# Attention and routed experts on one core: GpSimd's indirect transfers get compute operations between them, and TensorE signals a values product only once a query group

## The chip, the cores and the metric

The kernel runs on one core of a Trainium2 chip. A core has TensorE (PE), VectorE (DVE), ScalarE (ACT), GpSimd (POOL) and SyncE (SP), each with its own in-order program; they meet through semaphores. Transfers run on 16 DMA engines: SP and ACT issue plain ones, GpSimd issues the indirect ones (rows picked by a list of indices). The metric is the device time of the core in microseconds (us), median over runs; less is better.

## The reference

The input x is (1, 2048, 128), float32. It is layer-normalised, and two branches are added to x.

```python
xn = layernorm(x)
# attention: one head of 128, though scaled by 1/sqrt(8)
q, k, v = split(xn @ w_qkv.T); s = q @ k.T / sqrt(8)
attn = softmax(s) @ v @ w_proj.T + b_proj
# routed experts: 8, the best 2 for each token
h = xn @ W_in + b_in
top-2 of softmax(h @ W_gate + b_gate), renormalised to sum 1
eout[e] = relu(h @ W1[e] + b1[e]) @ W2[e] + b2[e]
ffn = (sum of the two experts' outputs by weight) @ W_out + b_out
out = x + attn + ffn
```

## The kernel before

**Tiling.** The 2048 tokens are NT = 16 tiles of 128. Attention goes by six groups of queries, of 256, 256, 512, 512, 256 and 256 (`GROUPS`). A group of 512 takes 16 steps, one of 256 takes 8, with two key tiles each; steps are numbered through, and s counts them from the fourth group on (`BASE_B` = 32). In a step TensorE makes the scores into one of three banks (`scores`), ScalarE takes the exponential (`step`: `ph` in rounded form and `pf` in full from the third group on, only `pf` before), VectorE takes the remainder `pl` (`low`), and TensorE multiplies by the values two steps later (`values(i - 2)`). Beside that, the maxima of the next group's scores are found by pairs: `pair` on TensorE, `pair_max` on VectorE, 4, 8, 8, 4 and 4 pairs, put at given steps by `PAIR_STEP`.

**Stages.** After normalisation and projection VectorE finds each token's two experts and its two rows in a table sorted by expert (`slots`). The first three groups of attention run while GpSimd sends each token's row of h into this table in HBM. Then the experts run as MT = 39 tiles of 128 rows, and the results go to a second table. Then the last three groups run, while GpSimd fetches each token's two rows of results (`z`), ScalarE multiplies the first by its gate (`weigh`, line 495), VectorE adds the second times its own (`combine`, line 742), and a block of four tiles is transposed, projected and added to x (`moe_transpose`, `cT_copy`, `moe_project`, `moe_add`, at the steps of `BLOCK_AT`). Product j is put at the step s given by `weighed_at`, 5 + 13(j+1)//8: s = 6, 8, 9, 11, 13, 14, 16 and so on up to 31.

**GpSimd's order.** 16 bias additions of one tile each to x (line 320), then the wait for `slots`; 16 indirect transfers (line 342, tiles 0 to 7 twice); the first four copies of an expert's weights into `wst` (line 334); 16 more indirect transfers; the 35 other copies, each when its buffer is free; then 32 indirect fetches (line 365).

**Signals.** TensorE raises `st_done` after each scores product, `pv_done` after each values product, `max_done` after a pair, and `q_done`, `row_done`, `out_done`, `proj_done`, `cT_done` and `wo_done` after what their names say. ScalarE's `step` waits for `st_done` and, because `ph`, `pf` and `pl` have three buffers, for `pv_done` of three steps back. TensorE's own order has values(i - 3) ahead of scores(i).

Of the kernel before, what the change touches and what calls it, by code (L numbers as in the profile page):

```python
# [7 lines left out]
ALU = mybir.AluOpType  # L8
# [4 lines left out]
def attention_moe_kernel(nc, x, w_qkv, w_proj, b_proj, w_in, b_in, w_gate, b_gate,  # L13
# [43 lines left out]

    BY_DVE = [2, 2, 3, 3]
    NORMED = [sum(BY_DVE[:r + 1]) for r in range(NR)]

    def group_of(i):
        return max(g for g in range(NG) if FIRST[g] <= i)
# [12 lines left out]
    with ctx:  # L75
# [199 lines left out]
        @block.gpsimd  # L275
        def _(pool):
            pool.memset(ident[:, 0:P], 0.0).then_inc(Z["consts"], 1)
            pool.memset(xn[:, :, 0:1], 1.0).then_inc(Z["consts"], 1)
            pool.memset(wvT[:, D:D + 2], 0.0).then_inc(Z["consts"], 1)
            pool.wait_ge(Z["consts"], 3)  # L280
            pool.affine_select(out=ident[:, 0:P], in_=ident[:, 0:P], compare_op=ALU.not_equal, fill=1.0,
                               base=0, pattern=[[-1, P]], channel_multiplier=1).then_inc(Z["consts"], 1)
            pool.wait_ge(Z["consts"], 4)
            pool.tensor_copy(less0[:, :], ident[:, 0:P]).then_inc(Z["consts"], 1)
            pool.tensor_copy(wvT[:, D:D + 1], ident[:, 0:1]).then_inc(Z["consts"], 1)
            pool.wait_ge(Z["consts"], 6)
            pool.memset(less0[0:1, 1:P], -1.0).then_inc(Z["consts"], 1)
            pool.memset(less0[0:1, 0:1], 0.0).then_inc(Z["consts"], 1)
            pool.wait_ge(Z["qkv_loaded"], 16)
            pool.tensor_tensor(wdiff[:, :, :], w_raw[:, 0:3, :], w_raw[:, 0:3, 0:1].to_broadcast([P, 3, D]),  # L290
                               ALU.subtract).then_inc(Z["wdiff_ready"], 1)

            pool.memset(first_tile[:, :, :], 1.0).then_inc(Z["consts"], 1)
            pool.iota(desc[:, :], pattern=[[-1, NE]], base=NE, channel_multiplier=0,
                      allow_small_or_imprecise_dtypes=True).then_inc(Z["consts"], 1)
            pool.iota(thr[:, :], pattern=[[SL, NT]], base=0, channel_multiplier=0,
                      allow_small_or_imprecise_dtypes=True).then_inc(Z["consts"], 1)
            pool.iota(tile_no[:, :], pattern=[[1, MS]], base=0, channel_multiplier=0,
                      allow_small_or_imprecise_dtypes=True).then_inc(Z["consts"], 1)
            pool.wait_ge(Z["consts"], 12)  # L300
            pool.wait_ge(Z["ones_ready"], 1)
            pool.affine_select(out=tri[:, :], in_=ones[:, :], compare_op=ALU.is_gt, fill=0.0,
                               base=0, pattern=[[1, P]], channel_multiplier=-1).then_inc(Z["consts"], 1)
            pool.affine_select(out=first_tile[:, :, :], in_=first_tile[:, :, :], compare_op=ALU.is_gt, fill=0.0,
                               base=0, pattern=[[0, NE], [1, NT]], channel_multiplier=0).then_inc(Z["consts"], 1)

            pool.wait_ge(Z["xn_ready"], NORMED[NR - 1])
            pool.wait_ge(Z["xn_act_ready"], NT - NORMED[NR - 1])
            for r in range(NR):
                at = slice(TB * r, TB * (r + 1))  # L310
                pool.tensor_copy(xn_hi[:, at, :], xn[:, at, :]).then_inc(Z["xnn_hi_ready"], 1)
                pool.wait_ge(Z["xnn_hi_ready"], r + 1)
                pool.tensor_tensor(xn_lo[:, at, :], xn[:, at, :], raw(xn_hi[:, at, :]), ALU.subtract).then_inc(Z["xnn_lo_ready"], 1)


            pool.wait_ge(Z["wlate_loaded"], 16 * 3)
            pool.tensor_tensor(bsum[:, 0, :], bsum[:, 0, :], bsum[:, 1, :], ALU.add).then_inc(Z["x_biased"], 1)
            pool.wait_ge(Z["x_biased"], 1)
            for j in range(NT):
                pool.tensor_tensor(x_sb[:, j, :], x_sb[:, j, :], bsum[:, 0, :], ALU.add).then_inc(Z["x_biased"], 1)  # L320

            experts = {}

            def load_experts(first, n):
                _, values = nc.values_load_multi_w_load_instructions(
                    texp[0:1, first:first + n], engines=[pool.engine], min_val=0, max_val=NE - 1,
                    skip_runtime_bounds_check_because="a count of experts that is clamped to the last one")
                experts.update({first + k: v for k, v in enumerate(values)})

            def stage(t):  # L330

                if t >= 4:
                    pool.wait_ge(Z["y_ready"], t - 3)
                pool.tensor_copy(wst[:, t % 4, :], wtab[:, bass.ds(experts[t], 1), :].rearrange("p a n -> p (a n)")  # L334
                                 ).then_inc(Z["staged"], 1)

            pool.wait_ge(Z["zeroed"], 16 * 3)
            pool.wait_ge(Z["slots_ready"], 1)

            def scatter(j):  # L340
                for c in range(TOPK):
                    pool.indirect_dma_start(out=slots_in, out_offset=bass.IndirectOffsetOnAxis(ap=slots[:, c, j:j + 1], axis=0),  # L342
                                            in_=hl[:, j, 0:D], in_offset=None).then_inc(Z["scattered"], 16)

            for j in range(NT // 2):
                scatter(j)
            pool.wait_ge(Z["experts_ready"], 1)
            pool.wait_ge(Z["tab_loaded"], 16 * (2 * NE + 1))
            pool.wait_ge(Z["wT_copied"], 5)
            load_experts(0, 8)  # L350
            for t in range(4):
                stage(t)
            for j in range(NT // 2, NT):
                scatter(j)
            for t in range(4, MT):
                if t % 8 == 0:
                    load_experts(t, min(8, MS - t))
                stage(t)

            pool.wait_ge(Z["staged"], MT)  # L360
            for h in range(4):
                pool.wait_ge(s_y[h], 16 * ((MT + 3 - h) // 4))
            for j in range(NT):
                for c in range(TOPK):
                    pool.indirect_dma_start(out=z[:, j, c, :], out_offset=None, in_=slots_out,  # L365
                                            in_offset=bass.IndirectOffsetOnAxis(ap=slots[:, c, j:j + 1], axis=0)
                                            ).then_inc(s_z[j], 16)

        @block.scalar
        def _(act):  # L370
# [58 lines left out]
            row(0)  # L429

            def step(i):
                act.wait_ge(Z["st_done"], i + 1)
                if i >= 3:
                    act.wait_ge(Z["pv_done"], i - 2)
                if i >= PLAIN:
                    act.activation(ph[:, i % 3, :], ps[:, st_bank(i), :], ACT.Exp).then_inc(Z["ph_done"], 1)  # L436
                act.activation(pf[:, i % 3, :], ps[:, st_bank(i), :], ACT.Exp).then_inc(Z["pf_done"], 1)  # L437

            def copy_u(g):
                n = SIZE[g]  # L440
                act.wait_ge(Z["pv_done"], FIRST[g + 1])
                if g >= 1:
                    act.wait_ge(Z["out_done"], FIRST_ROUND[g])
                act.activation(ut[:, 0:n].rearrange("e (p j) -> e j p", j=NT),
# [45 lines left out]
                else:  # L490
                    step(BASE_B)

            def weigh(j):
                act.wait_ge(s_z[j], 32)
                act.activation(z[:, j, 0, :], z[:, j, 0, :], ACT.Copy, scale=gate1[:, j:j + 1]).then_inc(Z["z_weighed"], 1)

            def cT_copy(b):
                act.wait_ge(Z["cT_done"], b + 1)
                if b >= 1:
                    act.wait_ge(Z["wo_done"], b)  # L500
                act.activation(cT[:, :], ps[:, MX, :], ACT.Copy).then_inc(Z["cT_copied"], 1)

            act.wait_ge(Z["gates_ready"], 1)
            for g in range(PRE, NG):
                for k in range(STEPS[g]):
                    s = FIRST[g] + k - BASE_B
# [1 line left out]
                    if s >= 1:  # L508
                        step(BASE_B + s)
                    beside(g, k)  # L510
                    for j in weighed_at(s):
                        weigh(j)
                    if s in BLOCK_AT:
                        cT_copy(BLOCK_AT[s])
            copy_u(NG - 1)
# [3 lines left out]
        def _(dve):  # L519
# [89 lines left out]
            def add_out(g):  # L609
                first = GROUPS[g][0] // P  # L610
                at = x_sb[:, first:first + TILES[g], :]
                dve.wait_ge(Z["proj_done"], FIRST_ROUND[g + 1])
                if g == 0:
                    dve.wait_ge(Z["x_biased"], 1 + NT)
                return dve.tensor_tensor(at, ps[:, MB, 0:SIZE[g]].rearrange("p (j e) -> p j e", e=D), at, ALU.add)  # L615

            every = (slice(None),) * 3
# [120 lines left out]

            def combine(j):

                dve.wait_ge(Z["z_weighed"], j + 1)
                dve.scalar_tensor_tensor(out=z[:, j, 0, :], in0=z[:, j, 1, :], scalar=gate2[:, j:j + 1],
                                         in1=z[:, j, 0, :], op0=ALU.mult, op1=ALU.add).then_inc(Z["c_ready"], 1)
# [31 lines left out]
        def _(pe):  # L775
# [112 lines left out]
            def values(i):  # L888
# [7 lines left out]
                if g < WHOLE:  # L896
                    pe.wait_ge(Z["pf_done"], i + 1)
                    for h, c in enumerate(keys(i)):
                        last = pe.matmul(dst, xn[:, c, :], pf[:, i % 3, cols(g, h)], start=(first and h == 0),  # L899
                                         stop=(final and h == CH[g] - 1))  # L900
                    last.then_inc(Z["pv_done"], 1)
                    return
                pe.wait_ge(Z["ph_done"], i - PLAIN + 1)
                if g == WHOLE:
# [5 lines left out]
                for h, c in enumerate(keys(i)):  # L910
                    last = pe.matmul(dst, xn_hi[:, c, :], pl[:, i % 3, cols(g, h)], start=False,  # L911
                                     stop=(final and h == CH[g] - 1))
                last.then_inc(Z["pv_done"], 1)

            def out_rows(g, r):

# [205 lines left out]
```

## Time and profile before

| | us |
|---|---|
| Median of 3 runs (303.79 to 306.73) | 306.6 |
| The profiled execution, device time | 305.5 |
| Its span (first to last instruction) | 303.7 |
| PE busy | 240.0 (79%) |
| DVE busy | 148.1 (49%) |
| ACT busy | 123.3 (41%) |
| POOL busy | 126.1 (42%) |
| POOL copies of weights, 39 | 44.8 |
| POOL indirect transfers out, 32 | 31.2 |
| POOL indirect fetches, 32 | 32.2 |
| The experts' first product on PE (L1010) starts, in the chain | 131.7 |

The profile is of one execution. "Busy" is time within instructions; waits, and the issuing of plain transfers, are not in it. A row of the timeline gives the start, the duration, the engine, the line, the operation and, in brackets, how long the engine was idle before it and what ended that. "Remote" there, and "another core or an unknown queue" in the chain, mean that the profile shows no releaser close enough in time; "issue" means that it shows nothing to wait for. An indirect transfer's row on POOL is the time in which it is issued, not the movement of its data. PEclk is the share of full speed that TensorE's clock was granted.

### The profile page before, as it was taken

Reading aid. Unit: us, or ns where it says so; the run is one execution under the profiler, and the core shown is the slowest. Engines: PE = TensorE matmul, PEld = TensorE weight load, DVE = VectorE, ACT = ScalarE, POOL = GpSimd, SP = SyncE. Lnnn points to the kernel's source line nnn. Section 1 sums busy time; section 2 is a strip of 40 time slices with the busy share of each in tenths; the row PEclk is TensorE's granted clock in tenths of the full one; section 3 lists DMA queues with packets and bytes.
Section 4 is the critical chain, followed back from the end, with each engine's and each line's share of the span. In section 5 each row is a group of like instructions: output and inputs, shape, how many; then the busy total and the mean of one; then the engine's idle time right before and its main releaser. Section 6 shows DMA issues by size and latency. Waiting matters only on the chain.

```text
span 303.7 us, 4614 instructions
## 1 busy us (share of the span) xinstructions
PE 240.0 (79%) x1590; PEld 216.2 (71%) x1590; DVE 148.1 (49%) x340; ACT 123.3 (41%) x291; POOL 126.1 (42%) x147
## 2 busy tenths in 40 slices
PE   8896969517279877988999999999984700879895
PEld 8895847406268656778999999998863500769794
DVE  5747773244142777534444444445780100586463
ACT  1552412120005554643444444445762100755672
POOL 4059337797730000004666666650777773000000
PEclk9999798957969999999999999999998775699999
DMA  6899001101121000001222222211121122000011
GB/s 197 318 314 324 21 17 53 52 17 52 54 67 37 0 0 0 2 0 37 70 71 72 69 67 74 71 53 38 43 55 50 48 76 42 0 0 2 35 37 35
DMA packets 23046, 19.53 MB, mean 64 GB/s; under 512 B 3280, under 2 KB 19696, under 8 KB 22768
## 3 DMA queue, kind: packets, MB, share of 16 engines
q1 hardware_dynamic: 20000, 14.71, 16.0%
q0 software_dynamic: 2048, 4.20, 4.9%
q10 hardware_dynamic: 976, 0.33, 0.4%
q8 instruction: 13, 0.21, 0.3%
q14 instruction: 9, 0.07, 0.1%
HBM read 10.97 MB, written 8.26 MB: 63 GB/s over the span
## 4 chain that ended last, share of the span: by engine, by line
PE 62%; another core or an unknown queue 14%; DVE 10%; ACT 7%; issue 4%; DMA 2%; ACTq 1%
PE ps L1024 12%; PE ps L1010 11%; DVE part_max L587 5%; PE ps L837 4%; PE ps L778 4%; PE ps L780 4%; PE ps L779 4%; PE ps L899 3%; PE ps L911 3%; PE ps L907 3%; PE ps L908 3%; PE ps L786 2%; ACT pf L437 2%; DMA w_raw<-in_L_attn_w_proj_dram 2%
## 5 line engine op out<-in xcount | busy, mean ns | idle before, releaser
L334 POOL COPY wst<-wtab 128x1156 f32 x39 | 44.8, 1153 | 76.2 <-DVE y_sb L725 76.2
L597 DVE TENSOR_TENSOR pl<-pf,ph 128x512 fp32r<-128x512 f32 x48 | 33.3, 693 | 52.6 <-ACT pf L437 49.0
L437 ACT ACTIVATE pf<-ps 128x512 f32<-128x512 f32 x64 | 38.0, 593 | 47.6 <-remote 18.2
L436 ACT ACTIVATE ph<-ps 128x512 fp32r<-128x512 f32 x48 | 28.7, 598 | 57.4 <-PE ps L780 29.8
L778 PE MATMUL ps<-q_hi,xnT_hi 128*128 128x256 f32 (+1 forms) x96 | 36.5, 380 | 18.7 <-ACT q_hi L422 18.7
L587 DVE TENSOR_REDUCE part_max<-ps 128x1 f32<-128x1024 f32 x32 | 38.9, 1222 | 22.6 <-remote 10.5
L837 PE MATMUL ps<-xnT_hi,q_hi 128*128 128x512 f32 x64 | 23.2, 449 | 28.5 <-DVE part_max L587 25.3
L1024 PE MATMUL ps<-wst,mid 128*128 128x128 f32 x312 | 41.3, 275 | 0.9 <-DVE x_sb L615 0.9
L1010 PE MATMUL ps<-xgT,wst 128*128 128x128 f32 x312 | 41.3, 275 | 0.0
L365 POOL DMA_INDIRECT wtab<-slots_out,slots x32 | 32.2, 1005 | 17.7 <-issue 9.4
L1024 PEld LDWEIGHTS ps<-wst,mid 128*128 128x128 f32 x312 | 38.0, 192 | 1.1 <-issue 1.0
L342 POOL DMA_INDIRECT slots_in<-hl,slots x32 | 31.2, 976 | 18.2 <-issue 9.3
L1010 PEld LDWEIGHTS ps<-xgT,wst 128*128 128x128 f32 x312 | 38.0, 192 | 0.1
L717 DVE TENSOR_SCALAR mid<-ps,wst 128x128 f32<-128x128 f32 x78 | 23.8, 346 | 29.0 <-PE ps L1010 29.0
L837 PEld LDWEIGHTS ps<-xnT_hi,q_hi 128*128 128x128 f32 x64 | 10.9, 200 | 34.4 <-DVE part_max L587 26.9
L778 PEld LDWEIGHTS ps<-q_hi,xnT_hi 128*128 128x128 f32 x96 | 20.0, 208 | 21.0 <-ACT q_hi L422 19.4
L779 PE MATMUL ps<-q_hi,xnT_lo 128*128 128x256 f32 (+1 forms) x96 | 32.1, 335 | 0.0
L780 PE MATMUL ps<-q_lo,xnT_hi 128*128 128x256 f32 (+1 forms) x96 | 31.9, 332 | 0.0
L477 ACT ACTIVATE mid<-ps,wst 128x128 f32<-128x128 f32 x78 | 24.4, 364 | 7.5 <-PE ps L1010 7.5
L470 ACT ACTIVATE xgT<-ps 128x128 f32<-128x128 f32 x39 | 10.9, 278 | 33.6 <-PE ps L998 33.6
L907 PE MATMUL ps<-ph,xn_hi 128*128 128x512 f32 (+1 forms) x64 | 22.2, 359 | 0.0
L908 PE MATMUL ps<-ph,xn_lo 128*128 128x512 f32 (+1 forms) x64 | 21.5, 347 | 0.0
(145 smaller groups left out, 360.7 us busy)
## 6 DMA issues: line engine op xcount, KB each, us to landing
wtab<-in_L_ffn_W_dram SPq DMA_DIRECT2D x16, 256.0 KB, 6.0
xg<-slots_in SPq DMA_DIRECT2D x39, 64.0 KB, 1.9
slots_out<-y_sb SPq DMA_DIRECT2D x39, 64.0 KB, 1.5
slots_in<-wst SPq DMA_DIRECT2D x2, 1024.0 KB, 5.0
x_sb<-in_L_attn_x_dram SPq DMA_DIRECT2D x4, 256.0 KB, 4.9
out_dram<-x_sb SPq DMA_DIRECT2D x3, 256.0 KB
wtab<-in_L_ffn_b_dram SPq DMA_DIRECT2D x1, 512.0 KB, 7.4
slots_in<-hl,slots POOLq DMA_INDIRECT x32
```

Of the source, the lines that this page charges most:

```text
L334: pool.tensor_copy(wst[:, t % 4, :], wtab[:, bass.ds(experts[t], 1), :].rearrange("p a n -> p (a n)")).then_inc(Z["staged"], 1)
L365: pool.indirect_dma_start(out=z[:, j, c, :], out_offset=None, in_=slots_out, in_offset=bass.IndirectOffsetOnAxis(ap=slots[:, c, j:j + 1], ...
L437: act.activation(pf[:, i % 3, :], ps[:, st_bank(i), :], ACT.Exp).then_inc(Z["pf_done"], 1)
L587: dve.tensor_reduce(part_max[:, g % 2, m // 2, m % 2:m % 2 + 1], ps[:, b:b + 2, :], AX.XY, ALU.max).then_inc(Z["max_read"], 1)
L597: dve.tensor_tensor(pl[:, i % 3, :], pf[:, i % 3, :], raw(ph[:, i % 3, :]), ALU.subtract).then_inc(Z["lo_done"], 1)
L778: pe.matmul(dst, lh, rh, start=start, stop=False)
L779: pe.matmul(dst, ll, rh, start=False, stop=False)
L780: return pe.matmul(dst, lh, rl, start=False, stop=stop)
L837: last = pe.matmul(ps[:, pair_bank(g, m) + b, :], q_hi[:, g % 2, P * t:P * (t + 1)], xnT_hi[:, at:at + BK], start=True, stop=True)
L907: pe.matmul(dst, xn_hi[:, c, :], ph[:, i % 3, cols(g, h)], start=(first and h == 0), stop=False)
L1010: last = pe.matmul(ps[:, 2 * (t % 2) + h, SL * (c % 2):SL * (c % 2 + 1)], wst[:, t % 4, P * c:P * (c + 1)], xgT[:, t % 2, :], start=True, ...
L1024: last = pe.matmul(ps[:, y_bank(t), 0:D], mid[:, t % 2, c, :], wst[:, t % 4, DM + D * c:DM + D * (c + 1)], start=(c == 0), stop=(c == HC - 1))
```

## The change

1. `BARE, UNTIED, STAGE_AT = 4, 2, [20, 23, 26, 29]`. Only 2 of the 16 bias additions stay ahead of the transfers. The other 14 follow transfers 4 to 17, one each.
2. The four first weight copies (and the waits and register loads before them) stand after transfers 20, 23, 26 and 29 instead of together after the 16th.
3. The gate product `weigh(j)` moves from ScalarE to GpSimd: each pair of fetches from the third on is followed by the product of the tile two before; the last two stand at the end. VectorE's `combine` now also waits for the fetch itself.
4. VectorE's `add_out` waits in every group for the biases of its own tiles, not in the first group for all of them.
5. ScalarE's `step` no longer waits for `pv_done`; TensorE raises `pv_done` after the last values product of a group only, 6 times in place of 64, and `copy_u` counts groups.

```diff
-            for j in range(NT):
+            def bias(j):
                 pool.tensor_tensor(x_sb[:, j, :], x_sb[:, j, :], bsum[:, 0, :], ALU.add).then_inc(Z["x_biased"], 1)
+            for j in range(UNTIED):
+                bias(j)
...
-            for j in range(NT // 2):
-                scatter(j)
-            pool.wait_ge(Z["experts_ready"], 1)
-            pool.wait_ge(Z["tab_loaded"], 16 * (2 * NE + 1))
-            pool.wait_ge(Z["wT_copied"], 5)
-            load_experts(0, 8)
-            for t in range(4):
-                stage(t)
-            for j in range(NT // 2, NT):
-                scatter(j)
+            for n in range(TOPK * NT):
+                j, c = n // TOPK, n % TOPK
+                pool.indirect_dma_start(out=slots_in, out_offset=bass.IndirectOffsetOnAxis(ap=slots[:, c, j:j + 1], axis=0),
+                                        in_=hl[:, j, 0:D], in_offset=None).then_inc(Z["scattered"], 16)
+                if UNTIED + n - BARE in range(UNTIED, NT):
+                    bias(UNTIED + n - BARE)
+                if n in STAGE_AT:
+                    if n == STAGE_AT[0]:
+                        pool.wait_ge(Z["experts_ready"], 1)
+                        pool.wait_ge(Z["tab_loaded"], 16 * (2 * NE + 1))
+                        pool.wait_ge(Z["wT_copied"], 5)
+                        load_experts(0, 8)
+                    stage(STAGE_AT.index(n))
...
+            def weigh(j):
+                pool.wait_ge(s_z[j], 32)
+                pool.tensor_scalar(z[:, j, 0, :], z[:, j, 0, :], gate1[:, j:j + 1], None, ALU.mult).then_inc(Z["z_weighed"], 1)
+            pool.wait_ge(Z["gates_ready"], 1)
             for j in range(NT):
                 for c in range(TOPK):
...
+                if j >= 2:
+                    weigh(j - 2)
+            weigh(NT - 2)
+            weigh(NT - 1)
...
             def step(i):
                 act.wait_ge(Z["st_done"], i + 1)
-                if i >= 3:
-                    act.wait_ge(Z["pv_done"], i - 2)
...
             def copy_u(g):
-                act.wait_ge(Z["pv_done"], FIRST[g + 1])
+                act.wait_ge(Z["pv_done"], g + 1)
...
-                    for j in weighed_at(s):
-                        weigh(j)
...
-                if g == 0:
-                    dve.wait_ge(Z["x_biased"], 1 + NT)
+                dve.wait_ge(Z["x_biased"], 1 + first + TILES[g])
...
             def combine(j):
+                dve.wait_ge(s_z[j], 32)
                 dve.wait_ge(Z["z_weighed"], j + 1)
...
-                    last.then_inc(Z["pv_done"], 1)
+                    if final:
+                        last.then_inc(Z["pv_done"], 1)
```

## Rows read from the trace of the kernel before

**Rows 1.** The page: the chain that ended last, by engine.
```profile
PE 62%; another core or an unknown queue 14%; DVE 10%; ACT 7%; issue 4%; DMA 2%; ACTq 1%
```

**Rows 2.** Windows: stretch, its length, busy us (x instructions) by engine, PEclk, DMA.
```profile
core 0: us, PE busy (x) PEld busy (x) DVE busy (x) ACT busy (x) POOL busy (x), PEclk, DMA share, GB/s
66.00:90.00 24.00, 13.76 (x54) 10.76 (x55) 9.71 (x13) 1.28 (x3) 16.30 (x17) 0.73 0.14 48
...
258.00:277.00 19.00, 15.67 (x101) 14.56 (x102) 12.71 (x23) 11.44 (x25) 0.00 (x0) 0.87 0.00 1
```

**Rows 3.** Timeline, first 16 indirect transfers: start, us, engine, line, operation.
```profile
53.35 0.40 PE L780 MATMUL ps<-xnT_lo,mm_hi 128*128 128x512 f32 x1
...
56.14 0.60 ACT L418 ACTIVATE q_hi<-ps 128x512 fp32r<-128x512 f32 x1 [0.82 <-remote]
...
56.77 0.69 DVE L581 TENSOR_TENSOR q_lo<-ps,q_hi 128x512 fp32r<-128x512 f32 x1 [6.50 <-ACT q_hi L418]
...
63.93 0.60 ACT L437 ACTIVATE pf<-ps 128x512 f32<-128x512 f32 x1 [7.19 <-remote]
64.65 1.23 DVE L587 TENSOR_REDUCE part_max<-ps 128x1 f32<-128x1024 f32 x1 [5.97 <-remote]
```

**Rows 4.** Timeline, second 16 indirect transfers.
```profile
76.20 0.61 PE L941 MATMUL ps<-wpT,o_sb 128*128 128x128 f32 x4
...
77.36 0.63 PE L837 MATMUL ps<-xnT_hi,q_hi 128*128 128x512 f32 x2
...
79.16 0.42 DVE L615 TENSOR_TENSOR x_sb<-ps,x_sb 128x256 f32<-128x256 f32 x1 [2.40 <-remote]
...
82.02 0.60 ACT L437 ACTIVATE pf<-ps 128x512 f32<-128x512 f32 x1 [8.40 <-remote]
...
84.15 1.23 DVE L587 TENSOR_REDUCE part_max<-ps 128x1 f32<-128x1024 f32 x1 [4.57 <-remote]
```

**Rows 5.** Timeline, PE and ACT while the results are fetched.
```profile
216.03 0.60 ACT L436 ACTIVATE ph<-ps 128x512 fp32r<-128x512 f32 x1 [0.73 <-PE ps L911]
...
218.36 0.40 ACT L495 ACTIVATE wtab<-wtab,gate 128x128 f32<-128x128 f32 x1
...
225.10 0.60 ACT L436 ACTIVATE ph<-ps 128x512 fp32r<-128x512 f32 x1 [0.73 <-PE ps L780]
...
227.34 0.66 PE L1057 MATMUL ps<-ident,wtab 128*128 128x128 f32 x4 [0.92 <-DVE wtab L742]
...
232.88 0.60 ACT L501 ACTIVATE cT<-ps 128x512 f32<-128x512 f32 x1 [2.43 <-remote]
...
233.53 2.08 PE L1065 MATMUL ps<-wo_sb,cT 128*128 128x128 f32 x8 [4.15 <-issue]
...
257.60 0.60 ACT L436 ACTIVATE ph<-ps 128x512 fp32r<-128x512 f32 x1 [19.09 <-remote]
...
259.13 0.57 ACT L436 ACTIVATE ph<-ps 128x512 fp32r<-128x512 f32 x1
```

**Rows 6.** Timeline of POOL: copies, biases, transfers.
```profile
1.70 0.29 POOL L284 COPY less<-ident 128x128 f32<-128x128 f32 x1
...
26.26 6.87 POOL L320 TENSOR_TENSOR x_sb<-x_sb,bsum 128x128 f32<-128x128 f32 x16
42.07 1.17 POOL L342 DMA_INDIRECT slots_in<-hl,slots  x1 [8.94 <-DVE slots L664]
...
62.49 4.42 POOL L334 COPY wst<-wtab 128x1156 f32 x4
67.08 0.97 POOL L342 DMA_INDIRECT slots_in<-hl,slots  x1 [0.17 <-issue]
...
211.91 1.00 POOL L365 DMA_INDIRECT wtab<-slots_out,slots  x1 [8.29 <-DMA slots_out<-y_sb]
...
252.56 0.95 POOL L365 DMA_INDIRECT wtab<-slots_out,slots  x1 [0.31 <-issue]
```

**Rows 7.** Timeline of DVE: one routing operation beside the biases, and after them.
```profile
30.94 0.52 DVE L632 TENSOR_TENSOR eq<-lg,top 128x128 f32<-128x128 f32 x1
...
33.63 0.29 DVE L639 TENSOR_TENSOR eq<-lg,top 128x128 f32<-128x128 f32 x1
```

More of the change, by code:

```diff
@@ L59, in attention_moe_kernel @@
     NORMED = [sum(BY_DVE[:r + 1]) for r in range(NR)]
+    BARE, UNTIED = 4, 2
+    STAGE_AT = [20, 23, 26, 29]
     def group_of(i):
@@ L338, in _ @@
             pool.wait_ge(Z["slots_ready"], 1)
[L340 to L343, printed above, removed]
-            for j in range(NT // 2):
-                scatter(j)
-            pool.wait_ge(Z["experts_ready"], 1)
-            pool.wait_ge(Z["tab_loaded"], 16 * (2 * NE + 1))
-            pool.wait_ge(Z["wT_copied"], 5)
-            load_experts(0, 8)
-            for t in range(4):
-                stage(t)
-            for j in range(NT // 2, NT):
-                scatter(j)
+            for n in range(TOPK * NT):
[11 more added lines that the diff above has]
+                    stage(STAGE_AT.index(n))
             for t in range(4, MT):
@@ L491, in _ @@
                     step(BASE_B)
-            def weigh(j):
-                act.wait_ge(s_z[j], 32)
-                act.activation(z[:, j, 0, :], z[:, j, 0, :], ACT.Copy, scale=gate1[:, j:j + 1]).then_inc(Z["z_weighed"], 1)
             def cT_copy(b):
@@ L501, in cT_copy @@
                 act.activation(cT[:, :], ps[:, MX, :], ACT.Copy).then_inc(Z["cT_copied"], 1)
-            act.wait_ge(Z["gates_ready"], 1)
             for g in range(PRE, NG):
@@ L912, in values @@
                                      stop=(final and h == CH[g] - 1))
-                last.then_inc(Z["pv_done"], 1)
+                if final:
+                    last.then_inc(Z["pv_done"], 1)
             def out_rows(g, r):
```

## The prediction, made before the changed kernel was run

> **What bounds the kernel now.** The first view is the chain of waits on the page. TensorE carries 62% of it, but 14% of the span, some 43 us, goes to a releaser that the profile cannot name [rows 1]. On one core no other core can be meant, so the second view is the timeline at those places. They all lie inside GpSimd's runs of indirect transfers.
>
> In the first run, TensorE ended the query projection at 53.75. ScalarE, free by then but for one exponential of 0.60, took it at 56.14. VectorE, idle for 5.97 us, began the maximum of a pair only at 64.65 [rows 3]. In the second run, TensorE ended a projection at about 76.8, the scores before 77.4 and a pair at 78.0; they were taken at 79.16 by VectorE, at 82.02 by ScalarE and at 84.15 by VectorE [rows 4]. Among the fetches, the transposes ended at 228.0 and ScalarE copied them at 232.88; one exponential later it stood for 19.09 us, until 257.60 [rows 5]. What ScalarE tells VectorE is not late: q_hi ended at 56.74 and VectorE began at 56.77 [rows 3]. Nor is what ScalarE tells TensorE: the copy ended at 233.48 and TensorE began at 233.53 [rows 5]. My reading: **what TensorE signals arrives late, and that only.**
>
> When? Transfers begin every 1.27 us (0.96 and a gap of 0.31) [rows 6]. The first run began at 42.07; the query projection at 53.75 was late, ten transfers in. The second began at 67.08 and the first late signal is that of 76.8, at the eighth. The fetches began at 211.91 and nothing is late up to 225.10, eleven transfers in [rows 4, 5, 6]. It ends when GpSimd turns to something else: the first weight copy began at 62.49, and ScalarE went on at 63.93; the last fetch ended at 253.51, and ScalarE went on at 257.60 [rows 3, 5, 6]. After the four copies the second run again had eight good transfers. So a long unbroken run starts it and other work on GpSimd stops it.
>
> **The change part by part.**
>
> *Biases and copies between the transfers out (14 and 4).* A bias is 6.87/16 = 0.43 us; behind it the gap is 0.17 in place of 0.30 [rows 6]. Each adds about 0.3 us, 14 x 0.3 = 4.2 us. The copies stay 4.42 us. The run now ends near 91, not 87.1. Nobody waits for it: the experts' first product is at 131.7 (table above), and would be near 115 if all below came true. The longest stretch with nothing between is four transfers ahead and then three, against a first late signal at eight. I take it that nothing is late any more. Then the pair's maximum comes at 53.75 + 0.60 (q_hi) + 1.91 (q_lo and three routing operations, 56.77 to 58.68) = 56.3 in place of 64.65: 8.3 us. In the second run it comes at 78.0 and not 84.15: 6.1 us. Together **14.4 us**, with 0 as the other end.
>
> *The biases off the stretch before 33 us.* VectorE's comparison took 0.52 beside them and 0.29 after them [rows 7]; five such operations give about 1 us. I count 0: TensorE comes to the prefix product, which waits for this, only in its own order, after four scores products. The other end is 1 us of gain. The same row prices the reverse: the biases, and 16 gate products, now run beside VectorE's later work. At 0.23 us for each meeting, with perhaps four meetings on the path, I count **-1 us**; with all 30 it is -7 us.
> The Trainium skill ("SBUF — State Buffer", Who interferes with whom) speaks against the change here: a VectorE operation with two inputs in SBUF and a GpSimd operation that reads SBUF exclude each other for the whole instruction. The trace agrees in direction; the 0.52 is not a full bias longer. By the rule the 16 products could hold VectorE for 16 x 0.29 = 4.6 us, and the sum would be 3.6 us worse.
>
> *Gate products between the fetches.* A product of 128x128 with one input is like the 0.29 us copy [rows 6]; the upper bound is the bias, 0.43. Six fetches stand bare; then come 0.29 and a gap of 0.17 for every two fetches. Product 0 ends at 211.91 + 6 x 1.30 - 0.3 + 0.3 = 219.7, and each further one 2.77 us later (two fetches of 1.0, gaps of 0.30 and 0.17, product 0.29): product 3 at 228.0, product 6 at 236.3. Before, the fourth product was in place for the transposes of 227.34 [rows 5]; they now come 1.1 us later. That is a new wait of VectorE, with the remainder of its next step, the values product and the transposes behind it. Products 4 to 6 come about when needed; from s = 16 on a product is due every 1.6 steps, and the 19 us from 258 to 277 [rows 2] held only eight steps, 3.8 us for a product against 2.77: the wait is gone.
> If nothing is late, ScalarE's steps go on at (225.10 - 216.03)/6 = 1.51 us. From 225.10 (s = 11) to s = 15 that is 6.0 us, plus 0.4 for the four transposes and 1.0 for the eight passes of the block's projection (2.08 at the low clock), plus the 1.1: step 15 at 233.6 in place of 259.13. Gain **25.5 us**. The other end: the lateness returns (rival 1).
>
> *Clock.* After the stalls TensorE was granted less: 0.73 in 66 to 90 with 13.76 us of work, 0.87 in 258 to 277 with 15.67 us [rows 2]. At full clock that is 3.7 and 2.0 us less work; the chain holds less than half of it. I take **2.4 us**, between 0 and 5.7.
>
> *Fewer signals, and no wait for pv_done.* The wait never binds: scores(i) stands behind values(i - 3) in TensorE's order. It leaves ScalarE one wait less a step, 0 us. ScalarE also loses 16 x 0.40 us, off the path. If signals are still late, about two in seven of those sent between s = 12 and 15 go; in rows that is 2/7 of 25.5 = 7 us, and a third of 14.4 = 5 us. With nothing late it is worth 0.
>
> *The x_biased waits.* At 1.56 us each from about 47 on, tiles 2 and 3 are biased by 51 and tiles 4 to 7 by 58. The addition for tiles 0 and 1 was at 79.16 [rows 4]; those for the others stand a group of steps behind it. 0 us.
>
> **Sum.** 14.4 + 25.5 + 2.4 - 1 = 41.3 us. The profiled execution (305.5, span 303.7) becomes 264.2. The median shown is 1.1 above that execution: 265.3. With a small allowance for signals that still wait a little, I say **266**.
>
> **Rivals.**
>
> *1. Cured among the transfers out, not among the fetches.* For: there the spacing is thin, 0.16 us more for a fetch, and they go on for 45 us; if the mean rate of transfers matters and not the unbroken run, only the first part is cured (rate down by a fifth against a fifteenth). Against: an unbroken run is two long after the first six. Time: 306.6 - 14.4 - 1.6 of clock, less 0 to 13 us of what thinner signals and some spacing give back: 277 to 291, middle 284.
>
> *2. Spacing does nothing, only the missing signals count.* Gain 7 + 5 = 12 us: 294.6, between 288 and 302. Against it: the stall ended 1.4 us after a copy began. The Trainium skill ("VectorE: DVE Perf Modes", The TRN2 errata) says that dense completion increments from several engines should be spaced; it gives no time. By this rule the thinned signals would do it all and the time would be the main one; nothing in this trace separates the two, and it moves no chance of mine.
>
> *3. The reading is wrong and the change does not do what it says.* ScalarE and VectorE might stall on something of their own, the fetching of instructions, say. For: the profile names no releaser. Against: VectorE moved at 79.16 while ScalarE stood until 82.02, and ScalarE stood twice with a handful of instructions between, before 232.88 and before 257.60 [rows 4, 5]. Time 303 to 309.
>
> *4. Slower: GpSimd stands at the gate products.* Product j waits for a fetch issued two pairs, 5.2 us, before. Were landing slower, GpSimd would stop 14 times and fetches, products and the last groups would slip. It turns into a loss where landing takes more than 5.2 + 41/14 = 8.1 us; at 9 us it costs 14 x 3.8 = 53 us against 41, that is 318. Against: ScalarE multiplied tile 0 at 218.36, 4.2 us after its second fetch had been issued at 214.2 [rows 5, 6], so it had landed; at that pace there is no stop.
>
> **How the numbers follow.** Main case 0.52 (own range 260 to 272: all meetings of VectorE with GpSimd cost 6 more, full clock gives 3 less). Rival 1 0.24, rival 2 0.10, rival 3 0.06, rival 4 0.05, other losses 0.03. The range 260 to 291 holds the main case, rival 1 and the lower end of rival 2. A measurement of this kernel tells about 1% from no change. Faster: 0.52 + 0.24 + 0.09 = 0.85; same: most of rival 3 and the end of rival 2, 0.07; slower: 0.08.
>
> **What would show it.** Right: no "unknown queue" share in the chain; the second group's first maximum near 56; ScalarE's idle time before step 14 under 1 us; the experts' first product near 115; PEclk near 1.0 in the stretches of rows 2; the last 32 fetches over some 44 us. Wrong: idle times of 2 us and more ended by "remote" among the fetches (rival 1) or everywhere (rival 2); POOL idle before its products (rival 4). The size would be wrong if VectorE, now beside GpSimd, becomes what every step waits for.

## The result, and the profile after

The changed kernel took 266.4 us (median of 4 runs, 266.31 to 270.92) against 305.2 us before (4 runs, the three shown and one beside the new kernel). The ratio is 0.8728, 95% interval 0.8654 to 0.8801: 12.7% less. The prediction was 266. Some executions of most kernels here are about 5 us longer than the others of the same kernel; the ratios leave them out, the medians in us hold them, of e5_fill_pair below only one of four was free of it, and the profiles of e5, e6_fill_clumped and e11_small_fill are of such long executions, whose extra time lies ahead of the first fetch.

The page of the changed kernel first: its chain of waits by engine, which answers to [rows 1], and its granted clock in 40 slices of 6.6 us.

```profile
PE 67%; DVE 12%; POOL 6%; ACT 5%; issue 5%; DMA 3%; ACTq 1%; POOLq 0%; DVEq 0%
```
```profile
PEclk9999898999999999999999999999999959999999
```

The unknown queue, 14% of the span before, is gone. POOL is new in the chain with 6%, and there is one slice at half the clock, about 211 to 218 us.

The windows of the changed kernel (stretch, length, busy time by engine, PEclk) answer to [rows 2]:

```profile
66.00:90.00 24.00, 20.08 (x103) 16.47 (x102) 13.50 (x18) 10.62 (x19) 20.46 (x22) 1.00 0.12 39
```

In the same 24 us TensorE does 103 products, not 54, at full clock and not 0.73. GpSimd is busier than before, 20.46 us against 16.30.

The timeline of VectorE and ScalarE in the changed kernel while the rows of h are sent out, to be held against [rows 3, 4]:

```profile
53.46 0.60 ACT L437 ACTIVATE q_hi<-ps 128x512 fp32r<-128x512 f32 x1
...
54.09 0.69 DVE L592 TENSOR_TENSOR q_lo<-ps,q_hi 128x512 fp32r<-128x512 f32 x1 [4.16 <-ACT q_hi L437]
...
55.83 1.22 DVE L598 TENSOR_REDUCE part_max<-ps 128x1 f32<-128x1024 f32 x1
...
65.77 0.42 DVE L625 TENSOR_TENSOR x_sb<-ps,x_sb 128x256 f32<-128x256 f32 x1
66.95 1.23 DVE L598 TENSOR_REDUCE part_max<-ps 128x1 f32<-128x1024 f32 x1 [0.76 <-PE ps L848]
```

The maximum of the first pair begins at 55.83 (64.65 before), and the one behind the addition to x at 66.95 (84.15 before). No idle time is ended by "remote".

Where the gain lies is read from GpSimd's first fetch, which stands at the border of the two stages. It was at 211.91 [rows 6] and is at 193.33: **18.6 us** ahead of it. From there to the end of the span it was 303.7 - 211.9 = 91.8 us and is 264.5 - 193.3 = 71.2 us: **20.6 us** behind it. The fetch stage of the changed kernel, the timeline of GpSimd, VectorE and TensorE:

```profile
193.33 0.99 POOL L380 DMA_INDIRECT wtab<-slots_out,slots  x1 [8.36 <-DMA slots_out<-y_sb]
...
209.84 0.95 POOL L380 DMA_INDIRECT wtab<-slots_out,slots  x1 [0.30 <-issue]
210.82 1.03 POOL L375 TENSOR_SCALAR wtab<-wtab,gate 128x128 f32<-128x128 f32 x1
```
```profile
208.47 0.39 DVE L753 SCALAR_TENSOR_TENSOR wtab<-wtab,gate 128x128 f32<-128x128 f32 x1 [2.09 <-POOL wtab L375]
...
211.96 0.39 DVE L753 SCALAR_TENSOR_TENSOR wtab<-wtab,gate 128x128 f32<-128x128 f32 x1 [0.58 <-POOL wtab L375]
```
```profile
212.41 1.11 PE L1070 MATMUL ps<-ident,wtab 128*128 128x128 f32 x4 [4.67 <-DVE wtab L753]
213.17 0.78 PE L919 MATMUL ps<-ph,xn_hi 128*128 128x512 f32 x1
```

TensorE's signals are not late here either. The loss is another: the fourth tile's gate product ends at 211.85, VectorE's sum at 212.35, and TensorE stood 4.67 us before the transposes. After that its clock was low: the values product takes 0.78 us where it takes 0.39 at full clock.

All groups of the gate product in one row (duration min/median/max in ns):

```profile
L375 POOL TENSOR_SCALAR wtab<-wtab,gate x16: 604/698/1157, 201.4 to 246.8; 128x128 f32<-128x128 f32 x16
```

### The profile page after: what moved, and what is told of

The parts are those of the page before. It is cut to its first block, busy times and chain, and to the rows that moved or that the text cites. A ratio compares the mean times of both kernels' runs of the same rounds, so it can differ in the third digit from the quotient of the medians.

```text
span 264.5 us, 4573 instructions
## 1 busy us (share of the span) xinstructions
PE 233.3 (88%) x1590; PEld 211.6 (80%) x1590; DVE 147.9 (56%) x340; ACT 119.0 (45%) x275; POOL 142.2 (54%) x163
## 3 DMA queue, kind: packets, MB, share of 16 engines
q1 hardware_dynamic: 20000, 14.71, 18.5%
q0 software_dynamic: 2048, 4.20, 5.8%
## 4 chain that ended last, share of the span: by engine, by line
PE 67%; DVE 12%; POOL 6%; ACT 5%; issue 5%; DMA 3%; ACTq 1%; POOLq 0%; DVEq 0%
PE ps L1037 13%; PE ps L1023 13%; DVE part_max L598 7%; PE ps L848 5%; POOL wtab L380 5%; PE ps L789 4%; PE ps L791 4%; PE ps L790 4%; PE ps L910 3%; PE ps L797 3%; PE ps L923 3%; PE ps L919 3%; PE ps L920 3%; DMA w_raw<-in_L_attn_w_proj_dram 2%; ACT pf L455 2%
## 5 line engine op out<-in xcount | busy, mean ns | idle before, releaser
L608 DVE TENSOR_TENSOR pl<-pf,ph 128x512 fp32r<-128x512 f32 x48 | 35.2, 733 | 34.4 <-ACT pf L455 33.4
L353 POOL DMA_INDIRECT slots_in<-hl,slots x32 | 32.8, 1024 | 21.8 <-DVE slots L674 14.8
L1037 PE MATMUL ps<-wst,mid 128*128 128x128 f32 x312 | 41.3, 275 | 0.9 <-DVE x_sb L625 0.9
L380 POOL DMA_INDIRECT wtab<-slots_out,slots x32 | 33.0, 1031 | 16.1 <-DMA slots_out<-y_sb 8.4
L1023 PE MATMUL ps<-xgT,wst 128*128 128x128 f32 x312 | 41.3, 275 | 0.0
L789 PE MATMUL ps<-q_hi,xnT_hi 128*128 128x256 f32 (+1 forms) x96 | 35.4, 369 | 0.5 <-ACT q_hi L441 0.5
L848 PE MATMUL ps<-xnT_hi,q_hi 128*128 128x512 f32 x64 | 21.8, 424 | 14.4 <-DVE part_max L598 13.9
L790 PE MATMUL ps<-q_hi,xnT_lo 128*128 128x256 f32 (+1 forms) x96 | 31.4, 327 | 0.0
L791 PE MATMUL ps<-q_lo,xnT_hi 128*128 128x256 f32 (+1 forms) x96 | 31.3, 326 | 0.0
L848 PEld LDWEIGHTS ps<-xnT_hi,q_hi 128*128 128x128 f32 x64 | 10.2, 191 | 19.8 <-DVE part_max L598 15.8
L789 PEld LDWEIGHTS ps<-q_hi,xnT_hi 128*128 128x128 f32 x96 | 19.1, 199 | 2.2 <-ACT q_hi L441 0.7
```

The costliest lines, as they stand in the source:

```text
L608: dve.tensor_tensor(pl[:, i % 3, :], pf[:, i % 3, :], raw(ph[:, i % 3, :]), ALU.subtract).then_inc(Z["lo_done"], 1)
L789: pe.matmul(dst, lh, rh, start=start, stop=False)
L790: pe.matmul(dst, ll, rh, start=False, stop=False)
L791: return pe.matmul(dst, lh, rl, start=False, stop=stop)
L848: last = pe.matmul(ps[:, pair_bank(g, m) + b, :], q_hi[:, g % 2, P * t:P * (t + 1)], xnT_hi[:, at:at + BK], start=True, stop=True)
L1023: last = pe.matmul(ps[:, 2 * (t % 2) + h, SL * (c % 2):SL * (c % 2 + 1)], wst[:, t % 4, P * c:P * (c + 1)], xgT[:, t % 2, :], start=True, ...
```

## Experiments

The theory at this point (S): an unbroken run of indirect transfers makes what TensorE signals arrive late, and other work on GpSimd stops that. Its rivals: the density of signals does it (G); or both parts of the change are needed. Pace below is the time from the start of one fetch to the next, from the 7th to the 32nd.

**e1_spacing_only: the change without its fifth part.**

```diff
             def step(i):
                 act.wait_ge(Z["st_done"], i + 1)
+                if i >= 3:
+                    act.wait_ge(Z["pv_done"], i - 2)
...
-                    if final:
-                        last.then_inc(Z["pv_done"], 1)
+                    last.then_inc(Z["pv_done"], 1)
```

> The changed kernel, but TensorE signals every values product again and ScalarE waits for it again: spacing without thinned signals. Theory S (an unbroken run of indirect transfers makes TensorE's signals late, other work on GpSimd stops it): nothing is late, so the signals cost nothing, 266 to 268 us. Theory G (it is the density of signals that makes them late, and leaving out two in seven cures it): late again, 290 to 303 us. If both parts are needed: 270 to 290 us, with idle times of 2 us and more ended by 'remote'.

Measured: ratio to before 0.8694 (0.8621 to 0.8766), the changed kernel's own being 0.8728. Span 265.1 against 264.5. No idle time is ended by "remote". From the first fetch to the end it takes 71.5 us, the changed kernel 71.2. The signals left out and the wait removed are worth nothing that can be measured once the transfers are spaced.

**e2_signals_only: only the fifth part, GpSimd as before.**

```diff
             def step(i):
                 act.wait_ge(Z["st_done"], i + 1)
-                if i >= 3:
-                    act.wait_ge(Z["pv_done"], i - 2)
...
-                last.then_inc(Z["pv_done"], 1)
+                if final:
+                    last.then_inc(Z["pv_done"], 1)
```

> The kernel before with only part 5 of the change: pv_done once a group, no wait for it in ScalarE's step. GpSimd's order is untouched. Theory S: the lateness stays, each late signal less in the queue gives back some: 294 us (288 to 302), with stalls of several us in both runs of transfers out and among the fetches. Theory G: 262 to 270 us.

Measured: 302.5 us, ratio 0.9884 (0.9814 to 0.9953). It is 1.2% faster, 3.6 us, not the 12 of my second rival, and just outside the 288 to 302 that I expected. The timelines of GpSimd, TensorE and ScalarE in this kernel show why:

```profile
209.02 1.00 POOL L365 DMA_INDIRECT wtab<-slots_out,slots  x1 [8.30 <-DMA slots_out<-y_sb]
```
```profile
233.16 0.49 PE L910 MATMUL ps<-pl,xn_hi 128*128 128x512 f32 x1 [0.48 <-issue]
...
255.00 0.58 PE L776 MATMUL ps<-q_hi,xnT_hi 128*128 128x256 f32 x1 [21.34 <-ACT q_hi L422]
```
```profile
63.70 0.60 ACT L435 ACTIVATE pf<-ps 128x512 f32<-128x512 f32 x1 [7.93 <-remote]
...
253.13 0.60 ACT L434 ACTIVATE ph<-ps 128x512 fp32r<-128x512 f32 x1 [20.46 <-remote]
```

The last of TensorE's products ended at 233.65, and ScalarE went on 19.5 us later; TensorE itself then stood still, because it waited for ScalarE. The stall hardly gets shorter with fewer signals. It ends 44.1 us after the first fetch; before it ended 45.7 us after it (257.60 - 211.91) [rows 5, 6].

**e3_bare_fetches: the changed kernel with the gate products back on ScalarE.**

```diff
-            def weigh(j):
-                pool.wait_ge(s_z[j], 32)
-                pool.tensor_scalar(z[:, j, 0, :], ...
...
-                if j >= 2:
-                    weigh(j - 2)
-            weigh(NT - 2)
-            weigh(NT - 1)
...
+            def weigh(j):
+                act.wait_ge(s_z[j], 32)
+                act.activation(z[:, j, 0, :], z[:, j, 0, :], ACT.Copy, scale=gate1[:, j:j + 1]).then_inc(Z["z_weighed"], 1)
```

> The changed kernel, but the gate products are back on ScalarE at their old steps, so the 32 fetches stand bare; the transfers out stay spaced. Theory S: the transfers out stay cured, and after about eleven fetches signals are late again: 5/7 of 25.5 us lost, less the 4.7 us that the transposes waited for the gate product: about 280 us (272 to 290), ScalarE idle 'remote' for 5 us or more after the tenth fetch. If the fetches need no spacing once signals are thin: 259 to 263 us.

Measured: 292.5 us (287.6 and 291.6 in the two executions that are not long), ratio 0.9456 (0.9356 to 0.9557), at the upper end of my 272 to 290 or beyond it. The lateness among the fetches is back, and in full: from the first fetch to the end it takes 92.4 us, and before it took 91.8. ScalarE's timeline:

```profile
225.63 0.60 ACT L445 ACTIVATE ph<-ps 128x512 fp32r<-128x512 f32 x1 [8.57 <-issue]
...
239.05 0.60 ACT L445 ACTIVATE ph<-ps 128x512 fp32r<-128x512 f32 x1 [12.04 <-remote]
```

Spacing is needed in the fetch stage by itself. Thin signals did not soften the loss.

**e4_tiny_fill: as e3, with 128 zeros after each pair of fetches.**

```diff
                                             ).then_inc(s_z[j], 16)
+                if j >= 2:
+                    pool.memset(scratch[:, j:j + 1], 0.0)
```

> As e3_bare_fetches, but GpSimd writes zeros into one unused column of SBUF (128x1) after each pair of fetches from the third on, where the gate product stood. If any operation of GpSimd's between two transfers is enough: nothing is late and the wait of 4.7 us for the gate product is gone too, 259 to 263 us. If it is the length of the gap that counts (0.1 us in place of 0.6 to 1.2 us): as e3_bare_fetches, 272 to 290 us.

Measured: 287.5 us, ratio 0.9378 (0.9316 to 0.9441), within the 272 to 290 of the second case. So theory S as I had put it is wrong: an operation after each pair of transfers is not enough. GpSimd's timeline in e4:

```profile
200.50 0.13 POOL L380 MEMSET scratch<- 128x1 f32 x1
200.82 1.06 POOL L376 DMA_INDIRECT wtab<-slots_out,slots  x1 [0.19 <-issue]
202.18 0.95 POOL L376 DMA_INDIRECT wtab<-slots_out,slots  x1 [0.30 <-issue]
203.13 0.11 POOL L380 MEMSET scratch<- 128x1 f32 x1
203.43 0.94 POOL L376 DMA_INDIRECT wtab<-slots_out,slots  x1 [0.19 <-issue]
```

The zeros lie inside the gap that is there anyway; the pace is 1.25 us, no slower than with none (1.27). That led to a new theory (R: the pace of the transfers counts) and its rival (L: it takes an operation that reads, or one that waits for a landed transfer, both of which the gate product does).

**e5_fill_pair, e7_fill_each, e6_fill_clumped: a longer fill, placed in three ways.** All three are e3 with

```diff
+            def fill(n=1):
+                for _ in range(n):
+                    if filled[0]:
+                        pool.wait_ge(Z["filled"], filled[0])
+                    pool.memset(scratch[:, :], 0.0).then_inc(Z["filled"], 1)
+                    filled[0] += 1
```

where scratch is 128x512 and unused: `fill()` after each pair from the third on (e5), `fill(4)` after every eighth fetch (e6), `fill()` after each fetch from the fifth on (e7).

> Gate products on ScalarE; GpSimd writes zeros into an unused 128x512 tile after each pair of fetches from the third on, some 0.5 us with no input and no wait for a transfer. The pace becomes about 1.43 us a fetch, between the 1.25 of e4_tiny_fill (late) and the 1.67 of the changed kernel (not late). Theory R (the mean pace counts: each transfer leaves work behind that drains at some rate between): 259 to 262 us if the limit is under 1.43, 270 to 283 if it is over. Theory L (a gap needs an operation that reads SBUF, or one that waits for a landed transfer): as e4_tiny_fill, 284 to 290.

> The zeros as in e5_fill_pair, but four times in a row after every eighth fetch: the same mean pace, eight bare fetches between. If what piles up drains in any pause (the first lateness before came after eight to eleven transfers): within 2 us of e5_fill_pair. If the pause must come at every second transfer at least: 275 to 290 us, late before each pause.

> The zeros after every fetch from the fifth on: about 1.65 us a fetch, the pace at which the biases spaced the transfers out. Theory R: nothing late, 260 to 264 us; the transposes' wait for the fourth tile shorter than the 4.7 us of the changed kernel. Theory L: 284 to 300 us.

Measured. e7: 260.4 us, ratio 0.8587 (0.8540 to 0.8633), pace 1.72. e5: 260.3 in its one undisturbed run (266.0, 266.0 and 265.0 in the others), pace 1.54 and not the 1.43 reckoned, no "remote" at all. e6: 268.9, ratio 0.8880 (0.8843 to 0.8918), between its two expected ranges; pace 1.53, with late signals again between its pauses. GpSimd and ScalarE in e6:

```profile
208.77 2.31 POOL L379 MEMSET scratch<- 128x512 f32 x4
```
```profile
221.18 0.37 ACT L444 ACTIVATE q_hi<-ps 1x256 fp32r<-1x256 f32 x1 [1.48 <-remote]
```

An operation that neither reads nor waits for a transfer does it (L falls). The mean pace counts, but not over eight transfers: in clumps of eight at the same mean, 8.6 us of e5's gain are lost, and from the first fetch to the end, where both profiles are of long executions, 8.2 us (73.2 against 65.0).

**e8_wait_only: no operation at all, GpSimd waits until each pair has landed.**

```diff
+                if j >= 2:
+                    pool.wait_ge(s_z[j], 32)
```

> Gate products on ScalarE; in place of an operation GpSimd only waits, after each pair from the third on, until that pair has landed: a pause of about 2 us with nothing executed, some 2.2 us a fetch. Theory R: nothing late, but fetches later, 268 to 276 us, the transposes waiting 5 to 8 us. If GpSimd must execute something between: late signals, 285 us and more.

Measured: 271.0 us, ratio 0.8945 (0.8883 to 0.9006), pace 2.13. No "remote". The pause alone is enough: nothing has to be executed. R holds. It is 10.6 us slower than e7; the fetches now last 64.5 us, and TensorE stands 2.85 us before one set of later transposes (I had expected 5 to 8). That the later fetches are the whole of that loss was argued from this and not tried.

**e11_small_fill: e7 with a fill of 128x128**, to narrow the limit.

> e7_fill_each with a fill of 128x128 in place of 128x512, about 0.2 us: some 1.31 us a fetch, against 1.25 (late, e4_tiny_fill) and 1.42 (not late, e5_fill_pair). Theory R with a limit near the lower pace: 259 to 261 us; with a limit near 1.4: late again, 265 to 285 us, beginning later than after 11 fetches.

Measured: ratio 0.9029 (0.8933 to 0.9124), some 274 us. The pace was not 1.31 as I had reckoned but 1.40, for some fetches took 1.2 to 1.5 us; the 1.42 that I gave for e5 was a reckoned figure too, and its trace has 1.54. Signals are late. GpSimd, TensorE and ScalarE:

```profile
198.29 0.99 POOL L385 DMA_INDIRECT wtab<-slots_out,slots  x1 [8.30 <-DMA slots_out<-y_sb]
```
```profile
234.31 0.28 PE L801 MATMUL ps<-q_lo,xnT_hi 128*128 128x256 f32 x1
...
239.15 1.09 PE L1080 MATMUL ps<-ident,wtab 128*128 128x128 f32 x4 [4.57 <-issue]
```
```profile
236.06 0.60 ACT L457 ACTIVATE ph<-ps 128x512 fp32r<-128x512 f32 x1 [5.77 <-PE ps L801]
...
244.62 0.60 ACT L457 ACTIVATE ph<-ps 128x512 fp32r<-128x512 f32 x1 [7.47 <-remote]
```

The scores that ended at 234.59 were taken at 244.62, 10.0 us late. This profile is of a long execution, but the two that are not long (272.3 and 275.2 us) lie at least 11.9 us above e7's median as well.

**e10_half_rows: e3 with 64 rows a fetch.** Half the rows of the experts' results are left out.

```diff
-                    pool.indirect_dma_start(out=z[:, j, c, :], ...
-                        in_offset=bass.IndirectOffsetOnAxis(ap=slots[:, c, j:j + 1], axis=0)
+                    pool.indirect_dma_start(out=z[0:P // 2, j, c, :], ...
+                        in_offset=bass.IndirectOffsetOnAxis(ap=slots[0:P // 2, c, j:j + 1], axis=0)
```

> e3_bare_fetches, but each fetch brings 64 rows of 128, the rest of z is left as it is (a part of the routed experts' result is left out). If the issue time of a fetch goes with its rows, fetches follow each other every 0.8 us or less, and the run of 32 is over in some 26 us. If what piles up goes with the rows: lateness as in e3_bare_fetches for half the time, or none where the issuing of 64 rows is slower in rows per us. If it goes with the number of transfers: lateness sooner than after 11 fetches' 14 us and at least as long a stall.

Measured: 292.3 us, ratio 0.9642 (0.9566 to 0.9718). A fetch of 64 rows takes 0.90 us, one of 128 took 0.95, so the run did not get short and the fetches' pace is 1.23. The stall is that of e3 (its first fetch is 4.8 us later than e3's, so times are counted from there):

```profile
198.22 0.93 POOL L375 DMA_INDIRECT wtab<-slots_out,slots  x1 [8.31 <-DMA slots_out<-y_sb]
...
237.25 0.90 POOL L375 DMA_INDIRECT wtab<-slots_out,slots  x1 [0.30 <-issue]
```
```profile
243.50 0.60 ACT L445 ACTIVATE ph<-ps 128x512 fp32r<-128x512 f32 x1 [7.12 <-remote]
```

It is the number of transfers, not their rows or bytes. The number of packets is not separated from it: the page counts 2048 for the 64 indirect transfers in either kernel, 32 for each.

**e9_out_bare: e7 with biases, transfers out and first copies in the order of before.**

> e7_fill_each, but the biases and the 32 transfers out in the order of the kernel before (all biases ahead, 16 bare transfers, four copies, 16 bare transfers). Theory R: the lateness among the transfers out comes back with what the profile showed of before, 14.4 us of delays and the clock, less what thinner signals give (e2_signals_only gave 3.6 in all): 260.4 + 16 = 276 us (273 to 280). If the two stages' gains do not simply add: outside of that.

Measured: 275.3 us, ratio 0.9093 (0.9024 to 0.9163), 15.0 us above e7, where 16 was expected. Within the noise the two stages' gains add.

**The fetch stage in one table.** "Release" is the step of ScalarE before which the last long stall ended, counted from the first fetch's start; "run" is from there to the end of the last fetch, and "to the end" from there to the end of the span, which leaves out what happened ahead of the fetches. The transfers out are spaced in all but the kernels marked "bare".

| kernel | pace, us | run, us | release, us | release / 32 | to the end, us | device time, us |
|---|---|---|---|---|---|---|
| e10_half_rows | 1.23 | 39.9 | 45.3 | 1.42 | 92.1 | 292.3 |
| e4_tiny_fill | 1.25 | 40.8 | 45.6 | 1.43 | 92.7 | 287.5 |
| e3_bare_fetches | 1.27 | 41.1 | 45.6 | 1.43 | 92.4 | 292.5 |
| e2_signals_only, bare | 1.27 | 41.1 | 44.1 | 1.38 | 90.2 | 302.5 |
| before, bare | 1.29 | 41.6 | 45.7 | 1.43 | 91.8 | 305.2 |
| e11_small_fill | 1.40 | 44.6 | 46.3 | 1.45 | 77.1 | about 274 |
| e6_fill_clumped | 1.53 | 47.6 | short stalls only | | 73.2 | 268.9 |
| e5_fill_pair | 1.54 | 48.2 | no stall | | 65.0 | 260.3 |
| changed kernel | 1.69 | 51.9 | no stall | | 71.2 | 266.4 |
| e7_fill_each | 1.72 | 53.2 | no stall | | 64.9 | 260.4 |
| e9_out_bare, bare | 1.72 | 53.2 | no stall | | 64.8 | 275.3 |
| e8_wait_only | 2.13 | 64.5 | no stall | | 74.5 | 271.0 |

The release moves by 2.2 us, from 44.1 to 46.3, while the end of the run moves by 4.7 us, from 39.9 to 44.6. It stands at 32 times 1.38 to 1.45 us. The first 16 transfers out of the kernel before say the same: from 42.07 to 64.65 is 22.6 us, 1.41 for each [rows 3, 6]; e2 and e9 have 22.6 us there too. The second 16 do not say it clearly: the last late signal came 17.1 us after their start before, 18.4 us in e9 and 22.5 us in e2, which is 1.07 to 1.40 for each. A reading that fits most of this is that something works each transfer off in some 1.4 us: GpSimd may hand them over faster; what is left grows; and until it is worked off, TensorE's signals get through seldom or not at all. This reading is not shown. What the something is, the traces don't show either, but it is not the movement of the rows: in the kernel before, the queue of the indirect transfers moved its last packet at 254.75, 1.24 us after the last fetch was issued, and ScalarE went on only at 257.60. I tried nothing that reads it directly.

## Why the prediction was right, point by point

**That only TensorE's signals are late, and only in GpSimd's runs.** Held in every kernel: each idle time ended by "remote" is of ScalarE or VectorE before an operation that reads what TensorE wrote, and it lies in or right behind a run of indirect transfers. There is none among fetches with a pace above 1.5 us, but for the three short ones of e6 with its clumps.

**"A long unbroken run starts it and other work on GpSimd stops it."** Right in its consequence, wrong as a mechanism. The step failed where I took "other work" for the cause: e4 has other work at every second fetch and is late, e8 has none and is not. The eight to eleven good transfers would be, by the reading above, the time in which the difference of pace adds up: 11 x (1.43 - 1.30) = 1.4 us, about one transfer. That is an estimate, and it leans on a reading that is not shown. The rival that I had given 0.24 because "the mean rate matters" had the right quantity. It was wrong only about the side of the limit on which the fetches would fall. With the gate product at my 0.29 us the pace would have been 2.77 / 2 = 1.39 us, close to that of e11, which was late: the product's real length carried the fetches over the limit, as far as one late kernel at 1.40 can tell. There the prediction was lucky.

**The transfers out, 14.4 us and 1.6 of clock.** Measured 18.6 us at the first fetch. The pair's maximum: 8.8 against 8.3. From there to the maximum behind the addition 8.4 more, against 6.1; 0.9 of that is VectorE's first gate operation, which took 1.16 us beside the weight copies and 0.22 away from them. The rest, 1.4, comes behind it. e9 and e7 give 15.0 us for this stage, measured without the gate products on GpSimd. Against 14.4 and 1.6 the stage gave 2.6 us more, of which 0.5 is the first maximum and 0.9 the gate operation; how much of the last 1.2 is clock was not separated.

**The run ends near 91 and nobody waits.** The last transfer out ended at 93.4, for the bias took 0.47 and some transfers 1.2 to 1.4. TensorE's first expert product, at 111.3, was not held up.

**The fetches, 25.5 us.** Measured 20.6, with the clock in it. The mis-sized term is the gate product. I priced it by a 0.29 us copy of the start-up, with 0.43 as upper bound. It took 0.60 to 1.16, median 0.70: 0.60 to 0.63 even with no remainder operation of VectorE's beside it, and more beside one (below). So a tile took (244.31 - 202.15) / 12.5 = 3.37 us and not 2.77, product 3 ended 18.5 us after the first fetch and not 16.1, and the transposes came after a wait of 4.67 us where I had 1.1. e7 shows the price: with the product on ScalarE and a fill in its place, at an even slower pace of fetches, its profiled span is 5.7 us less (258.8 against 264.5), 64.9 us from the first fetch to the end, 26.9 less than before. TensorE there waits 0.92 us before the transposes:

```profile
209.32 0.66 PE L1080 MATMUL ps<-ident,wtab 128*128 128x128 f32 x4 [0.92 <-DVE wtab L763]
```

The sum for undisturbed fetches was good to a few per cent; the new wait was not.

**VectorE beside GpSimd, -1 us.** The remainder operation now takes 0.733 us on average, 0.693 before: 48 x 0.04 = 1.9 us in all. Most of it falls on two remainders beside weight copies. VectorE and GpSimd in the changed kernel:

```profile
89.11 2.16 DVE L608 TENSOR_TENSOR pl<-pf,ph 128x512 fp32r<-128x512 f32 x1
```
```profile
89.56 1.16 POOL L343 COPY wst<-wtab 128x1156 f32 x1
```

The remainder took 2.16 us beside a weight copy of 1.16; it ended 0.55 after the copy. The Trainium skill ("SBUF — State Buffer", Who interferes with whom) says that such a pair exclude each other for a whole instruction. The trace agrees here, though the remainder had begun 0.45 us before the copy. It agrees for the gate products too. The third stood alone, and the fourth, of 1.03 us at 210.82 (above), met a remainder:

```profile
207.75 0.62 POOL L375 TENSOR_SCALAR wtab<-wtab,gate 128x128 f32<-128x128 f32 x1
```
```profile
210.71 0.68 DVE L608 TENSOR_TENSOR pl<-pf,ph 128x512 fp32r<-128x512 f32 x1
```

The eight products with no remainder beside them took 0.60 to 0.63 us, the eight with one 0.76 to 1.16: 0.34 more on average, 2.7 us in all. Each of those eight ended 0.38 to 0.48 us after the remainder. Among the fetches it was thus mostly the other way round than I had it. I had counted what GpSimd costs VectorE, 1 us, or 4.6 for the products by the rule; the products cost the remainders about 0.2 us, and the remainders held the products. By an estimate from these rows, 1.3 of the 2.4 us by which the fourth product was later than forecast are the products' own length (four times 0.62 - 0.29), and 0.6 are VectorE's doing.

**Fewer signals, 0 us when nothing is late.** Right (e1). My price of 12 us for the case that all is late was three times too high (e2: 3.6): I had taken the signals for a queue served one by one, but the long stall ends at nearly the same time however few signals wait (44.1 us after the first fetch against 45.7).

**The sum.** 39.2 us of span against 41.3 forecast. The transfers out gave 2.6 us more than their terms and the fetches 4.7 us less (20.6 against 25.5 and 0.8 of clock, less the 1 for VectorE). The median of 266.4 against 266 owes something to these two and to the small allowance. Of the signs that I named, the unknown queue's share, the second group's first maximum, the experts' start and the clock in 66 to 90 us came out; ScalarE's idle time before step 14 was 2.28 us and not under 1, with TensorE named as its releaser, and the 32 fetches took 51.9 us and not 44.

**A version that is faster than both.** e7_fill_each, 260.4 us, ratio to before 0.8587 (0.8540 to 0.8633). Its interval lies below that of the changed kernel (0.8654 to 0.8801); the two were not run side by side.

## What to carry to other kernels

Where ScalarE and VectorE wait for TensorE longer than its products take, and GpSimd is issuing many small indirect transfers one after another, look at their pace before anything else; here 1.54 us from start to start, evenly spread, kept the signals on time and 1.40 did not. A pause at each transfer or each second one does it, by work or by a wait, and useful work is only the better filler while it is shorter than what its consumer can wait for. Price an operation that moves to another engine by a row in which that engine has the same neighbours, not by one from the start-up.

## What the runs showed of the hardware that was not expected

TensorE's signals alone are held up, in e2 until 19.5 us after its last product had ended, by indirect transfers that fill a fraction of the DMA engines' time (0.14 in the stretch of [rows 2]); ScalarE's signals to VectorE and TensorE pass in 0.03 and 0.05 us in the same runs [rows 3, 5]. The long stalls among the fetches end 1.38 to 1.45 us times the number of transfers after the first, with 64 rows or 128, while GpSimd hands one over every 1.23 to 1.40 us and is never held back itself. An indirect fetch of 64 rows takes 0.90 us to issue and one of 128 rows 0.95, so there is little to gain from making them smaller. A GpSimd product of 128x128 takes 0.62 us by itself and up to 1.16 us beside VectorE's remainder operation.
